# Second layer: values multiplied in pieces of 512 query columns on every second beat, instead of 256 on seven beats

## The reference, cut to what matters

```python
qkv = x @ W_qkv + b_qkv                                  # 16 heads of 8 features
bias = slopes[:, None, None] * minimum(j - i, 0)          # alibi
scores = einsum('bhtd,bhsd->bhts', q, k) * scale + bias
w = softmax(scores, axis=-1)
y = einsum('bhts,bhsd->bhtd', w, v)                       # the values, weighted
return y.transpose(0, 2, 1, 3).reshape(B, T, C) @ W_proj + b_proj
```

## Time and profile before

| | us |
|---|---|
| median of 3 runs | 1198.96 (1197.5 to 1201.12) |
| profiled execution | 1204.42 |
| its span | 1202.7 |
| mean granted TensorE clock | 0.948 of full speed |

### The profile page before, as it was taken

One profiled execution on the slowest core, in us unless ns is written; L12 is line 12 of the kernel. 1 busy time (PEld: TensorE's weight loads), 2 busy tenths in 40 slices (PEclk: granted clock), 3 DMA queues, 4 the chain that ended last, 5 costly groups with the idle time before them and its releaser, 6 DMA issues. The chain is left out here.

```text
span 1202.7 us, 24028 instructions
## 1 busy us (share of the span) xinstructions
PE 1055.7 (88%) x8917; PEld 569.9 (47%) x8924; DVE 836.1 (70%) x1393; ACT 769.5 (64%) x1398; POOL 565.5 (47%) x759
## 2 busy tenths in 40 slices
PE   4789999999955999999999659988999999996885
PEld 2233443434323888888888513333333333333553
DVE  2667777777724666676666478788788887952986
ACT  1367777777742655555554348878789889883552
POOL 4345556555350011101110256766667767552876
PEclk9699999999976999999999869999999999998998
DMA  6422221122000000000000041202112112001001
GB/s 177 140 102 75 70 69 38 48 74 75 13 29 17 1 2 1 1 1 0 0 1 1 23 127 28 64 12 74 28 48 65 38 48 64 12 22 38 19 18 35
DMA packets 47494, 51.11 MB, mean 42 GB/s; under 512 B 11586, under 2 KB 40907, under 8 KB 46876
## 3 DMA queue, kind: packets, MB, share of 16 engines
q1 hardware_dynamic: 47388, 49.69, 14.5%
HBM read 16.62 MB, written 2.64 MB: 16 GB/s over the span
## 5 line engine op out<-in xcount | busy, mean ns | idle before, releaser
L590 ACT ACTIVATE at_E<-at_Sb 128x512 f32<-128x512 f32 x832 | 448.2, 598 | 113.9 <-PE at_Sb L464 109.2
L650 DVE TENSOR_REDUCE at_mx<-at_Mb 128x2 f32<-128x1024 f32 x256 | 296.9, 1217 | 51.9 <-PE at_Mb L429 50.8
L512 PE MATMUL at_Ob<-at_E,VP 128*32 128x256 f32 (+2 forms) x2816 | 212.1, 374 | 4.3 <-ACT Oev L598 2.2
L464 PE MATMUL at_Sb<-at_QP,at_KP 64*128 64x512 bf16 (+3 forms) x1024 | 202.9, 344 | 11.5 <-ACT at_full_k L561 3.6
L751 POOL TENSOR_TENSOR at_E<-at_E,at_factor 128x512 f32<-128x512 f32 x128 | 162.4, 1272 | 96.1 <-ACT at_E L590 86.5
L429 PE MATMUL at_Mb<-at_KP,at_QP 62*128 62x512 bf16 (+3 forms) x1024 | 175.6, 357 | 28.9 <-DVE at_mx L650 20.1
L653 DVE TENSOR_REDUCE at_mx<-at_Mb 128x2 f32<-128x768 f32 (+1 forms) x128 | 138.4, 1089 | 75.9 <-PE at_Mb L429 74.9
L762 POOL TENSOR_SCALAR_AFFINE_SELECT at_E<-at_E 128x512 f32<-128x512 f32 x128 | 79.9, 637 | 96.3 <-ACT at_E L590 95.9
L1032 ACT ACTIVATE ex_th<-ex_z 128x512 f32<-128x512 f32 x104 | 65.9, 633 | 84.1 <-DVE ex_z L1146 82.8
L429 PEld LDWEIGHTS at_Mb<-at_KP,at_QP 62*128 62x128 bf16 x1024 | 44.3, 93 | 152.9 <-issue 76.6
L1155 DVE TENSOR_TENSOR ex_hh<-ex_Rb,ex_th 128x512 f32<-128x512 f32 x104 | 71.9, 692 | 60.4 <-ACT ex_th L1032 55.8
(11 more groups left out here) (170 smaller groups left out, 1592.5 us busy)
## 6 DMA issues: line engine op xcount, KB each, us to landing
at_QP<-at_q SPq DMA_DIRECT2D x96, 128.0 KB, 2.4
at_KP<-at_k SPq DMA_DIRECT2D x96, 128.0 KB, 2.4
ctxN<-Oev SPq DMA_DIRECT2D x16, 256.0 KB, 2.9
denB<-rdram SPq DMA_DIRECT2D x64, 64.0 KB
gates<-gates_dram SPq DMA_DIRECT2D x1, 2048.0 KB, 7.4
at_QP<-at_nrow SPq DMA_DIRECT2D x128, 4.0 KB
out<-x SPq DMA_DIRECT2D x8, 256.0 KB, 2.3
w_raw<-in_w SPq DMA_DIRECT2D x2, 832.0 KB, 6.3
```

The costliest lines, as they stand in the source:

```text
L464: return pe.matmul(out[:, at:at + SEQ - q0], KP[p0:p0 + ROWS_H, b % 2, 2 * g + a, kt * P:(kt + 1) * P], QP[p0:p0 + ROWS_H, b % 2, 2 * g + ...
L512: last = pe.matmul(Ob[VW * i:VW * (i + 1), 0, q0:q1], weights_of(b, G, kt, i, q0), moving, start=(kt == 0 and q0 == 0), stop=False, skip_g ...
L590: nc.scalar.activation(dst, src, ACT.Exp).then_inc(s["s_read"], 1)
L650: v.tensor_reduce(mx[:, G % 2, :, t % 2, t // 2], src, AX.X, ALU.max).then_inc(s["m_read"], 1)
```

## The change

The values of one key tile are no longer split into two halves on two beats. All 512 columns of a tile are multiplied on one even beat; the odd beats have none. The counts that ScalarE waits for (`CH_DONE`) are adapted to four pieces per group.

```diff
         CHUNKS = ({5: ((0, 0, 256),), 6: ((0, 256, 512),), 7: ((1, 128, 512),), 8: ((3, 384, 512),), 9: ((2, 256, 512),)}
                   if causal else
-                  {6: ((0, 0, 256), (0, 256, 512)), 7: ((1, 0, 256),), 8: ((1, 256, 512),), 9: ((2, 0, 256),),
-                   10: ((2, 256, 512),), 11: ((3, 0, 256),), 12: ((3, 256, 512),)})
+                  {6: ((0, 0, 512),), 8: ((1, 0, 512),), 10: ((2, 0, 512),), 12: ((3, 0, 512),)})
         NCH = sum(len(c) for c in CHUNKS.values())
...
-        CH_DONE = (2, 4, 5) if causal else (2, 4, 6, 8)
+        CH_DONE = (2, 4, 5) if causal else (1, 2, 3, 4)
```

## The result

The changed kernel takes 1221.18 us (median of 4 runs, 1217.75 to 1227.92) against 1200.04 for the kernel before. The ratio is 1.019, 95% interval 1.013 to 1.025: slower by 21 us where 24.4 were forecast. One run of the kernel before (3167.63 us), one of those timed beside the runs on odd beats (1249.34) and one of the changed kernel with the last edit (1680.33) stand far above the rest; they are in the medians and not in the ratios. The profiled execution took 1222.87 us with a span of 1221.2, so 18.4 more than the profiled one before. Weight loads fell from 8924 to 8156, by the 768 that were forecast, and the time still rose.

The account below looks back on a forecast made before the run. Three engines near their limit, TensorE pacing regular beats; the timeline decides. Five full batches at +3.24 us, plus 2.54, 2.84 and 2.79 for the others, give +24.4: 1198.96 + 24.4 = 1223.4 us, range 1204 to 1236.

Parts of the forecast that it names:

- The loop of two beats: Odd beat plus next even beat: score waits for the exponential's bank, then values; 2.60 us instead of 2.22, +0.38.
- Fewer pieces: 0: Value matmuls, 40 to 28 a group: a cut costs nothing visible, so dropping cuts gains 0.
- The rival in which the saved turns pay: TensorE stays the bound and 23 us of saved turns between scores and values come off: 1176 us; chance 0.09.
- the 0.24 per stretch: TensorE's cost beside the columns for each stretch of values; three of seven go, 0.7 us per group, 23 us in all.
- the three specimens: Beats 5 to 7, 13 to 15, 29 to 31, already without values then with 512 columns: 2.60 us, no change.
- the copies on beat 4: ScalarE's two copies on beat 4: that pair forecast at 2.85 us, between 2.66 and 3.09.
- the fills at 0.43: Pairs with v, ln, q or k projection: longer values ahead of the fill ScalarE awaits, +0.43 each.
- The VectorE rival: VectorE paces regular pairs at 2.35 us, nothing at the fills, 6 us in all: 1205 us; chance 0.08.
- the wash: Saved turns count where TensorE is late and nearly offset the 3.24 a batch: +3 us, 1202 us; chance 0.04.
- The stretch of beats 15 to 23: Statistics, context product and output projection, VectorE pacing: +0.3 us, from 0.38 before beat 17 less 0.1; ends 0 and 0.9.
- the clock rival: One more fall of TensorE's clock in each batch adds 8 to 14 us: 1231 to 1237 us; chance 0.11.
- general fall: TensorE's clock halving throughout; not expected, as new regular pairs keep TensorE working some 2 of 2.6 us.

Follow-up runs that it names:

- the runs on odd beats: Changed kernel with its four 512-column pieces on odd beats instead of even ones: 1213.18 us, ratio 1.0118 to the kernel before.
- the last edit: Two small VectorE instructions given to GpSimd in the second layer; against the kernel before: 1196.45 us there, 1222.18 us in the changed kernel.
- the second experiment: Changed kernel with the values placed between the two scores on even beats of the second layer: 1214.14 us, ratio 1.0119 to the kernel before.

## Why the prediction was right

**The loop of two beats.** Right in each link: 0.65, 0.32, 1.00 and 0.64 against 0.63, 0.32, 1.01 and 0.64. That the bank's wait closes it rests on the second experiment: with the values ahead of the waiting score, regular pairs fell to 2.40, though the scores of even beats no longer run side by side.

**Fewer pieces: 0.** Right; with 40 matmuls on the same beats 1221.46. The rival in which the saved turns pay is dead: it said 1176. By the rows, the 0.24 per stretch is saved and waited away. The two scores of the even beat, which are meant to run side by side, start at 887.88 and 888.51, the second after its wait for the exponential; without these 0.63 the pair of 2.61 would take 1.98, and two regular beats of before took 2.22. That is an estimate from these rows; the busy time of TensorE's records doesn't show the saving (44.57 us of the batch from 862.65, and 44.50 before).

**The terms.** By the starts of exponentials in the batch shown, new against forecast (before in brackets):

| stretch of the batch | forecast | measured | by |
|---|---|---|---|
| 31 to 5 | 8.05 | 920.70 - 912.72 = 7.98 (7.35) | +0.63 |
| 7 to 9, v | 4.11 | 877.25 - 873.22 = 4.03 (3.68) | +0.35 |
| 9 to 13 | 5.45 | 882.66 - 877.25 = 5.41 (4.93) | +0.48 |
| 15 to 23, output projection | 12.87 | 898.17 - 885.25 = 12.92 (12.57) | +0.35 |
| 23 to 29, ln, q, k | 12.04 | 910.11 - 898.17 = 11.94 (10.75) | +1.19 |
| the batch | 50.34 | 50.07 (47.10) | +2.97 |

2.97 against 3.24 (the rows above sum to 3.00; the three specimens, now 2.59, 2.59 and 2.61, give back 0.03). The terms that were mis-sized are the copies on beat 4, taken as 0.25 and measured 7.98 - 3 x 2.61 = 0.15, and the fills at 0.43, measured 0.35 to 0.42. The VectorE rival is ruled out by pairs of 2.61 where it said 2.35, the wash by the total where it said 1202.

The stretch of beats 15 to 23 came out at +0.35 against +0.3 by luck. The working lets only what lies ahead of beat 17 add. The pairs 15-17 and 17-19 both grew, from 2.22 to 2.61, and the next, 19-21, shrank from 3.13 to 2.75: two terms that the prediction doesn't have, and they cancel.

**The sum over the phase.** From the first exponential of the phase to the last, in the two profiled executions:

| part | forecast | measured |
|---|---|---|
| first batch, to its beat 31 | +2.54 | 46.80 - 45.59 = +1.21 |
| five full batches | +16.2 | 250.33 - 241.69 = +8.64 |
| seventh batch | +2.84 | 45.87 - 43.02 = +2.85 |
| last batch | +2.79 | 46.18 - 40.08 = +6.10 |
| sum | +24.4 | +18.8 |

Behind these numbers are three things that the forecast doesn't have.

*Two long batches before.* The forecast took one clean batch of the kernel before for all. Three of its five full batches took 47.1, but two took 49.99 and 50.41 (from 761.52 and from 811.51), 6.2 us more together. Without them the five would give +14.84. The excess of the first, 2.89, lies in three places. The pairs 11-13 and 13-15 are 0.60 longer: VectorE's reciprocal waits 1.34 for the DMA that brings the softmax sums (`den`), which it doesn't in the clean batch at 877:

```profile
778.27 0.56 DVE L200 RECIPROCAL rden<-den 128x64 f32<-128x64 f32 x1 [1.34 <-DMA den<-Oev]
```
```profile
877.24 0.54 DVE L200 RECIPROCAL rden<-den 128x64 f32<-128x64 f32 x1
```

The pair 19-21 is 1.26 longer (4.39 against 3.13): VectorE's first small instruction takes 1.26 us. GpSimd, VectorE and the weight load behind them in this batch, then GpSimd and VectorE in the clean one:

```profile
788.88 1.27 POOL L751 TENSOR_TENSOR at_E<-at_E,at_factor 128x512 f32<-128x512 f32 x1
```
```profile
788.91 1.26 DVE L640 TENSOR_SCALAR at_nmean<-at_mv 128x4 f32<-128x4 f32 x1
```
```profile
791.42 0.10 PEld L429 LDWEIGHTS at_Mb<-at_KP,at_QP 62*128 62x128 bf16 x2 [1.90 <-DVE at_mx L650]
```
```profile
888.58 0.17 DVE L640 TENSOR_SCALAR at_nmean<-at_mv 128x4 f32<-128x4 f32 x1
...
888.69 1.27 POOL L751 TENSOR_TENSOR at_E<-at_E,at_factor 128x512 f32<-128x512 f32 x1
```

With GpSimd's product 0.03 us ahead, VectorE's instruction lasts until that product is over; with the product 0.11 us behind, 0.17. VectorE paces this stretch, so the 1.1 us are on the path. And the pair 21-23 is 1.05 longer: TensorE's longer wait was followed by the half clock of the earlier trace rows. The other long batch has the same three parts (a wait of 1.47 for the DMA and 0.72, then 1.23, then 1.37). The changed kernel has none of them in these batches. Its reciprocal waits for the DMA 0.01 at most, and GpSimd's product starts 0.54 behind the small instruction, which takes 0.17 in all six batches:

```profile
891.10 0.17 DVE L639 TENSOR_SCALAR at_nmean<-at_mv 128x4 f32<-128x4 f32 x1
```
```profile
891.64 1.27 POOL L750 TENSOR_TENSOR at_E<-at_E,at_factor 128x512 f32<-128x512 f32 x1 [0.48 <-ACT at_E L589]
```

The slower timetable thus gives back a loss of the old one. The Trainium skill ("SBUF — State Buffer", SBUF: two separate sides) describes a port pair shared by VectorE and GpSimd that belongs for a whole instruction to whichever starts first, for VectorE only with instructions of certain kinds. The 1.26 and 0.17 us agree with it; that this instruction is of such a kind no run here shows apart from these times.

*A fall of the clock in the last batch.* Two pairs of the changed kernel's profile take 3.60 and 3.69 there, and TensorE's clock is half from 1092.9 to 1099.7:

```profile
1092.90:1096.30 3.40, 3.22 (x20) 0.72 (x19) 0.00 (x0) 1.87 (x5) 2.09 (x3) 0.50 0.00 0
```
```profile
1092.13 2.06 ACT L589 ACTIVATE at_E<-at_Sb 128x512 f32<-128x512 f32 x4 [2.50 <-PE at_Sb L463]
1095.73 2.06 ACT L589 ACTIVATE at_E<-at_Sb 128x512 f32<-128x512 f32 x4 [1.53 <-PE at_Sb L463]
1099.42 2.06 ACT L589 ACTIVATE at_E<-at_Sb 128x512 f32<-128x512 f32 x4 [1.63 <-PE at_Sb L463]
```

In the profile of the kernel with pieces of 256, of the same time and beats, the same two pairs take 2.40 each (1091.79, 1094.19, 1096.59), and its last batch is 3.65 longer than before, not 6.10. So 2.5 us here belong to this one execution; that is all of the clock rival (8 to 14 us) that came. The remaining 3.65 are more than 2.79.

*The first batch* lost 1.21 and not 2.54. In the kernel before its half clock lasted from 716.7 to 727.0, in the changed one from 717.5 to 724.3. That may be the reason; it isn't shown.

So it is luck that the 6.2 us of the two long batches are just what the profiled pair lacks to 24.4; the other differences nearly cancel. For the unprofiled runs there is no trace. There the medians differ by 21.1, and by 25.7 with the two instructions moved, and 24.4 lies between.

**The clock.** I expected no general fall. Between the half clocks of the first and the last batch the changed kernel has none, where the kernel before has the one of the earlier trace rows and another from 843.1 to 846.5. The changed kernel's row:

```profile
724.50:1092.80 368.30, 328.70 (x2842) 114.06 (x2838) 295.79 (x316) 292.23 (x579) 235.73 (x297) 1.00 0.15 41
```

What stays open: why the DMA of the softmax sums is late in some batches and not in others, and whether its lateness is what sets the order of the two engines. In the kernel before, the one with tile 3 gathered and the one with fills first, the nine batches with the long instruction had waited 0.39 to 1.47 for it, the other six that have this DMA 0 to 0.39. The kernel before without the small instructions still has such a wait (1.10, at 774.55), and its batch takes 47.27 instead of 46.79.

## What to carry to other kernels

Where an engine must wait for a buffer before it may go on to a large block of work, the block's length adds to the chain of whoever fills that buffer; a kernel may already hold a beat that looks like the new timetable, as here, and its measured length was a good forecast for all. Merging work to save switches only pays if the saved time isn't waited away in front of the same buffer: here by the estimate 23 us of TensorE's work were saved, and the time rose by 21. Before trusting a total, compare all repeats of a batch, in both kernels: a loss of the old timetable can vanish with the change, a single execution can have one of its own, and wrong parts can sum to a right total.

## What the hardware showed that I had not expected

A VectorE instruction on 128x4 elements took 0.17 us or 1.26 to 1.27 us, and nothing between, in six batches of each of ten profiled kernels. All nine long ones began 0.03 us after the start of a GpSimd product of 1.27; the short ones began 0.10 us or more before it. So 0.1 us between two engines decided it: two of six batches in the kernel before, three of six with tile 3 gathered, four of six with the fills first, none in the changed kernel.

The start of the phase shows the same with another partner and a longer lead. Each of two profiled executions, before and after, has one such case; this is the one before. The instruction and the one behind it last until 0.02 us after a GpSimd memset that had begun 1.41 us ahead of the first:

```profile
683.89 2.66 POOL L769 MEMSET at_VD<- 128x3072 f32 x1
```
```profile
685.30 1.27 DVE L640 TENSOR_SCALAR at_nmean<-at_mv 128x4 f32<-128x4 f32 x1
685.38 1.20 DVE L641 TENSOR_SCALAR at_ve<-at_mv 128x4 f32<-128x4 f32 x1
```
